# Last batch tile of a DLRM tower: the previous tile's late stages in the turn phase, and two column chunks multiplied ahead of the third one's turn

## What is computed

```python
e = jnp.stack([tbl_f[ids[:, f]] for f in range(27)], axis=1)   # 2048 x 27 x 128
inter = jnp.einsum('bfd,bgd->bfg', e, e)[:, triu_i, triu_j]     # 351 pairs
h = jnp.concatenate([e.reshape(B, -1), inter, dense_ctx], axis=1)  # 3456 + 351 + 16
h = jnp.maximum(h @ W_top1 + b_top1, 0.0)                       # 512
h = jnp.maximum(h @ W_top2 + b_top2, 0.0)                       # 256
y = h @ W_top3                                                  # 1
```

## Time and profile before

| | us |
|---|---|
| median of 3 runs | 601.06 (599.7 to 602.52) |
| the profiled execution | 602.09 |
| its span, first to last instruction | 600.0 |
| TensorE busy | 537.2 (90% of the span) |
| VectorE busy | 349.6 (58%) |
| ScalarE busy | 233.9 (39%) |
| GpSimd busy | 418.9 (70%) |
| granted TensorE clock, mean | 0.989 of full |
| chain that ended last: TensorE, VectorE, ScalarE | 69%, 18%, 2% |

### The profile page before, as it was taken

The page is one execution under the profiler, slowest core; times in us unless marked ns, Lnnn a source line. Parts: engine busy times, 40 slices in busy tenths (PEclk is TensorE's granted clock), DMA queues, the critical chain, the costliest instruction groups (busy, mean ns, idle before and its releaser), DMA issues.

```text
span 600.0 us, 7903 instructions
## 1 busy us (share of the span) xinstructions
PE 537.2 (90%) x2576; PEld 480.6 (80%) x2576; DVE 349.6 (58%) x1165; ACT 233.9 (39%) x717; POOL 418.9 (70%) x438
## 2 busy tenths in 40 slices
PE   0757899998999999899999999999999999999896
PEld 0547788897988889798888879888888988888774
DVE  2653827558383746748274664828366483837854
ACT  2543335162433526143352615344261524335341
POOL 4777777777777777777777777777777777777000
PEclk9987899999999999999999999999999999999999
DMA  7673222122222212122222222221222212222000
GB/s 229 193 255 98 52 54 53 50 54 53 54 53 53 53 49 53 50 54 51 51 54 54 52 54 52 50 54 52 54 52 54 53 50 52 54 54 54 10 0 1
DMA packets 19435, 37.80 MB, mean 63 GB/s; under 512 B 7636, under 2 KB 8660, under 8 KB 19396
## 3 DMA queue, kind: packets, MB, share of 16 engines
q0 software_dynamic: 13824, 28.34, 18.4%
q1 hardware_dynamic: 5284, 8.72, 4.5%
q10 hardware_dynamic: 288, 0.26, 0.2%
HBM read 37.28 MB, written 0.01 MB: 62 GB/s over the span
## 4 chain that ended last, share of the span: by engine, by line
PE 69%; DVE 18%; POOL 4%; issue 4%; DMA 2%; ACT 2%; DVEq 0%
PE ps_acc L222 18%; PE ps_acc L223 14%; PE ps_acc L224 13%; DVE g_buf L487 9%; PE ps_gram L247 8%; PE ps_acc L259 8%; DVE g_buf L481 6%; PE ps_t L209 5%; POOL emb L196 4%; DVE emb_x L471 2%; PE ps_late L296 1%; DMA emb<-in_tbl,idx 1%; DMA idx<-in_ids 1%; PE ps_late L255 1%; ACT g_buf L423 1%
## 5 line engine op out<-in xcount | busy, mean ns | idle before, releaser
L196 POOL DMA_INDIRECT emb<-in_tbl,idx x432 | 418.3, 968 | 136.2 <-issue 129.5
L222 PE MATMUL ps_acc<-w_hi,emb_x 128*128 128x512 f32 x432 | 211.0, 488 | 21.4 <-DVE emb_x L471 21.4
L481 DVE COPY g_buf<-ps_gram 32x112 f32<-32x112 f32 x512 | 138.3, 270 | 91.1 <-PE ps_gram L247 81.0
L223 PE MATMUL ps_acc<-w_lo,emb_x 128*128 128x512 f32 x432 | 174.8, 405 | 0.0
L224 PE MATMUL ps_acc<-w_hi,emb_x 128*128 128x512 f32 x432 | 174.0, 403 | 0.0
L423 ACT ACTIVATE g_buf<-ps_gram 32x112 f32<-32x112 f32 x512 | 130.8, 256 | 91.7 <-PE ps_gram L247 87.2
L222 PEld LDWEIGHTS ps_acc<-w_hi,emb_x 128*128 128x128 f32 x432 | 130.7, 303 | 33.7 <-issue 21.2
L471 DVE TENSOR_TENSOR emb_x<-ps_t,emb_x 128x512 fp32r<-128x512 f32 (+1 forms) x112 | 74.5, 666 | 142.6 <-ACT emb_x L384 142.2
L223 PEld LDWEIGHTS ps_acc<-w_lo,emb_x 128*128 128x128 f32 x432 | 135.2, 313 | 2.6
L384 ACT ACTIVATE emb_x<-ps_t 128x512 fp32r<-128x512 f32 (+1 forms) x112 | 63.8, 583 | 180.3 <-PE ps_t L209 179.9
L224 PEld LDWEIGHTS ps_acc<-w_hi,emb_x 128*128 128x128 f32 x432 | 131.7, 305 | 1.0
(11 more groups left out here) (26 smaller groups left out, 119.5 us busy)
## 6 DMA issues: line engine op xcount, KB each, us to landing
g_buf<-in_W_top SPq DMA_DIRECT2D x27, 256.0 KB, 4.2
emb<-in_tbl,idx POOLq DMA_INDIRECT x432, 2.5
w_cols<-in_W_top SPq DMA_DIRECT2D x1, 512.0 KB
w<-in_W_top SPq DMA_DIRECT2D x1, 512.0 KB
w_cols<-in_W_top SPq DMA_DIRECT2D x1, 222.0 KB
idx<-in_ids SPq DMA_DIRECT2D x1, 216.0 KB, 5.4
b_rows<-in_b_top ACTq DMA_DIRECT2D x1, 128.0 KB, 4.9
w_rows<-in_W_top ACTq DMA_DIRECT2D x1, 128.0 KB, 6.0
```

Source lines behind the costliest of these rows:

```text
L196: pool.indirect_dma_start(out=emb[:, f * D:(f + 1) * D], out_offset=None, in_=tables[f], in_offset=bass.IndirectOffsetOnAxis(ap=idx[:, t, ...
L222: pe.matmul(acc, emb_part(0, f), w_hi[:, f, :], start=(f == 0), stop=False)
L223: pe.matmul(acc, emb_part(0, f), w_lo[:, f, :], start=False, stop=False)
L481: last = dve.tensor_copy(target, source)
```

## The change

It touches the last tile alone. On TensorE the late stages of tile 14 leave their places between the gram units (before units 2, 6, 10 and 14): the turn of its columns goes ahead of the turn of group 5, their product behind that turn and two multiplies, the turn of its hidden layer behind the turn of group 6, and layer 2 ahead of unit 10. ScalarE takes tile 14's columns ahead of split 5, its ReLU ahead of split 6, and the copy of the turned hidden layer behind that. VectorE packs tile 14's pairs one group earlier. The tile's own multiplies are dealt out anew: two each ahead of units 0, 3 and 6. The wait for s_h2 moves from behind the remaining multiplies to ahead of them. At the end eight multiplies, the turn of chunk 0, one multiply, the turn of chunk 1, two multiplies, the products of chunks 0 and 1, then turn and product of chunk 2.

```diff
--- before.py
+++ after.py
@@ -269,12 +269,10 @@
                     last = turn_chunk(n, ps_late[:, n * P:(n + 1) * P])
                 last.then_inc(s_cols_t, 1)
 
-            def turn_last_columns(t):
-
-                pe.wait_ge(s_h2, t)
-                for n in range(NCC):
-                    pe.wait_ge(s_cols, t + 1 + n)
-                    turn_chunk(n, ps_gram[:, n, 0:P]).then_inc(s_cols_t, 1)
+            def turn_last_chunk(t, n):
+
+                pe.wait_ge(s_cols, t + 1 + n)
+                turn_chunk(n, ps_gram[:, n, 0:P]).then_inc(s_cols_t, 1)
 
             def multiply_columns(t):
                 pe.wait_ge(s_cols_out, t + 1)
@@ -284,11 +282,11 @@
                     last = multiply_chunk(t, n)
                 last.then_inc(s_acc, 1)
 
-            def multiply_last_columns(t):
-                for n in range(NCC):
-                    pe.wait_ge(s_cols_out, t + 1 + n)
-                    last = multiply_chunk(t, n)
-                last.then_inc(s_acc, 1)
+            def multiply_last_chunk(t, n):
+                pe.wait_ge(s_cols_out, t + 1 + n)
+                last = multiply_chunk(t, n)
+                if n == NCC - 1:
+                    last.then_inc(s_acc, 1)
 
             def turn_h1(t):
                 pe.wait_ge(s_h1, t + 1)
@@ -347,24 +345,34 @@
                 for _ in range(count):
                     multiply(t, todo.pop(0))
 
-            for g, count in ((2, 4), (3, 2), (4, 2), (5, 1), (6, 1)):
-                turn_group(t, g)
-                multiply_next(count)
+            turn_group(t, 2)
+            multiply_next(4)
+            turn_group(t, 3)
+            multiply_next(2)
+            turn_group(t, 4)
+            multiply_next(2)
+            turn_columns(t - 1)
+            turn_group(t, 5)
+            multiply_next(2)
+            multiply_columns(t - 1)
+            turn_group(t, 6)
+            turn_h1(t - 1)
             for k in range(UNITS):
-                if k == 2:
-                    turn_columns(t - 1)
-                if k == 6:
-                    multiply_columns(t - 1)
+                if k in (0, 3, 6):
+                    multiply_next(2)
                 if k == 10:
-                    turn_h1(t - 1)
-                if k == 14:
                     layer_2(t - 1)
-                if k in (3, 5, 8, 9, 12, 13):
-                    multiply_next(1)
                 gram_unit(t, k)
-            multiply_next(len(todo))
-            turn_last_columns(t)
-            multiply_last_columns(t)
+            pe.wait_ge(s_h2, t)
+            multiply_next(len(todo) - 3)
+            turn_last_chunk(t, 0)
+            multiply_next(1)
+            turn_last_chunk(t, 1)
+            multiply_next(2)
+            multiply_last_chunk(t, 0)
+            multiply_last_chunk(t, 1)
+            turn_last_chunk(t, 2)
+            multiply_last_chunk(t, 2)
             turn_h1(t)
             layer_2(t)
 
@@ -443,16 +451,15 @@
                 for k in range(0, UNITS, 2):
                     take_blocks(t, k)
             t = TILES - 1
-            for g in range(NG):
+            for g in range(5):
                 split_group(t, g)
+            take_columns(t - 1)
+            split_group(t, 5)
+            relu_h1(t - 1)
+            split_group(t, 6)
+            take_h1(t - 1)
             for k in range(0, UNITS, 2):
                 take_blocks(t, k)
-                if k == 4:
-                    take_columns(t - 1)
-                if k == 8:
-                    relu_h1(t - 1)
-                if k == 12:
-                    take_h1(t - 1)
             take_last_columns(t)
             relu_h1(t)
             take_h1(t)
@@ -549,10 +556,10 @@
             layer_3(t - 2)
             split_group(t, 3)
             add_parts(t - 1)
+            pack_pairs(t - 1, 0, 10)
             split_group(t, 4)
-            pack_pairs(t - 1, 0, 10)
+            pack_pairs(t - 1, 10, NF - 1)
             split_group(t, 5)
-            pack_pairs(t - 1, 10, NF - 1)
             split_group(t, 6)
             for k in range(1, UNITS, 2):
                 take_blocks(t, k)
```

## The result

The changed kernel takes 605.61 us in the median of 6 runs (601.95 to 608.45), the kernel before 601.11 in 6. The ratio is 1.0071 with a 95% interval of 1.0045 to 1.0096: slower, by 0.7%. Forecast were 603.7 us and a range of 601.0 to 606.7. The profiled execution took 605.6 us with a span of 603.7.

The account below looks back on a forecast made before the run. VectorE's last block copy, plus 10.9 us to the end of the columns product, was taken to set the end. That product ending at 595.8 instead of 593.2 gave +2.6 us: 603.7 on the median's basis, range 601.0 to 606.7.

Parts of the forecast that it names:

- first place: TensorE's 2.6 us wait at 560.7 for tile 14's packed columns; a clock fall behind it priced at 1.5 us.
- Part 1: Turn phase: TensorE waits 2.6 us for tile 14's packed columns; gram unit 0 starts at 571.0, against 564.40.
- Part 2: Gram phase: VectorE's last block copy ends at 583.5, 1.2 us later than 582.34.
- Part 3: Wait for s_h2 ahead of the multiplies: TensorE idles 2.0 us, counted at 0 because chunk 0 is packed only at 589.8.
- Part 4: End of the last tile: TensorE has a backlog, and the columns product ends at 595.8, against 593.2.
- The sum: Whole kernel: +2.6 us on the profiled 602.09 gives 604.7, or 603.7 on the basis of the median.
- the likeliest case: The forecast itself: 603.7 us, from the order alone with no clock fall; chance 0.50.
- rival (a): TensorE's clock falls behind one or both long waits in the last tile: 605.2 or 606.7 us; chance 0.32.
- the second place: Stretch 579.8 to 584.0: TensorE issues three gram units and idles 3.5 us; a clock fall there priced at 1.5 us.
- (b): Nothing changes: gram phase nearer the copies' pace, last copy between 580.9 and 582.3, median 601.1 to 602.5; chance 0.13.
- (c): Faster: VectorE runs the gram phase without a gap, last copy before 580.9; 598.0 us; chance 0.05.

Follow-up runs that it names:

- changed, again: The changed kernel run again, unaltered, as base of the other experiments: median 606.28 us, ratio 1.0089 to the kernel before.
- wait for s_h2 late: The changed kernel with the wait for s_h2 moved from ahead of the last eleven multiplies to ahead of the hidden layer's turn: 604.94 us, ratio 1.0072.
- old end: The changed kernel's turn and gram phase with the kernel before's end: eleven multiplies, wait for s_h2, three turns, three products: 601.74 us, ratio 1.0014.
- second wait filled: The changed kernel plus 11 unread matmuls of 512 columns behind gram units 12, 14 and 15: 603.52 us, ratio 1.0039.
- both filled: The changed kernel with 11 unread matmuls behind gram units 12, 14, 15 and ten ahead of the turn of tile 14's columns: 603.26 us, ratio 1.0055.
- first filled: The changed kernel with only the ten unread matmuls ahead of the turn of tile 14's columns: 605.34 us, ratio 1.0079.
- before, new end: The kernel before with only the changed kernel's TensorE end, from the wait for s_h2 to chunk 2's product: 603.44 us, ratio 1.0034.
- before, wait early: The kernel before with only the wait for s_h2 moved ahead of the eleven multiplies: 602.37 us, ratio 1.0019.
- staggered end: The kernel before, ending: eleven multiplies, turns of chunks 0 and 1, product 0, turn 2, products 1 and 2, then wait for s_h2: 600.65 us, ratio 0.9988.
- with layer 3 late: The staggered end plus VectorE's layer 3 of tile 14 moved behind the last packs: 600.53 us, ratio 0.9997 to the kernel before.
- waits used: Staggered end and late layer 3, plus four of the tile's own multiplies moved into TensorE's four waits: 600.76 us, ratio 1.0004 to the kernel before.
- waits used, filled: Waits used, plus seven unread matmuls ahead of chunk 0's turn; on another chip 724.98 us against 725.95 for the kernel before, ratio 0.9931.

## Why the prediction was right, and where not

Each stretch is from one profiled execution, in us.

| kernel | stretch expected, clock at full | measured | clock fell in it |
|---|---|---|---|
| before | | 46.7 | no |
| changed, first profile | 49.3 | 51.9 | 6.8 us |
| changed, again | 49.3 | 49.4 | no |
| wait for s_h2 late | 49.3 | 49.5 | no |
| old end | 47.9 | 47.9 | no |
| second wait filled | 49.3 | 51.1 | 3.4 us, first place |
| both filled / first filled | 49.4 / 49.4 | 49.5 / 49.5 | no |
| before, new end | 48.1 | 49.9 | 3.4 us |
| before, wait early | 47.6 | 47.9 | no |
| staggered end | 46.0 | 46.1 | no |
| with layer 3 late | 45.4 | 46.2 | no |
| waits used | 44.9 | 47.0 | 3.4 us |
| waits used, filled (another chip) | 45.2 | 45.3 | no |

**Part 1** held to 0.2 us: wait 2.51 for 2.6, gram unit 0 at 571.15 for 571.0.

**Part 2** held: last copy at 583.5, as walked unit by unit, though the waits ahead of units 13 and 15 were 0.70 and 0.30 us for 0.95 and 0.6. What it costs by itself is the 1.2 us of the kernel with the old end.

**Part 3** held, with a wait of 1.75 us for 2.0: moved late, the wait for s_h2 gives back nothing (49.5 beside 49.4), since TensorE stands at chunk 0 instead. What is left for it to cost in the changed order is the clock, and with 3 of 6 runs marked when it stands late and 9 of 12 when it stands early, the runs are too few to tell how much of that is the wait's. On the kernel before, the same early wait costs 1.2 us.

**Part 4** held: TensorE issues the last turn behind four records of L259 and doesn't wait for VectorE. In the changed order the new end costs 1.6 us (47.9 to 49.5). Put on the kernel before, it costs 1.6 as well without the clock, but 1.2 of them are the early wait. That two chunks multiplied early would win where TensorE has no backlog was worked out in the prediction and not run; one chunk multiplied early, with all eleven multiplies ahead of the turns, gave 0.6 us of stretch (46.7 to 46.1). The multiplies put behind the turns are such a backlog.

**The sum**, +2.6, was measured as 2.7 where the clock held. The direction was right and the range holds the time, but the likeliest case was not the commonest: I gave rival (a) 0.32, and 9 of the changed kernel's 12 runs show its mark. The median of 605.6 lies beside the 605.2 of (a) with one fall, not beside the forecast's 603.7, so the range holds it thanks to the rival's share of it. The fall was at the second place that (a) names: on the clock of the rows before it lasts from 582.9 to 589.7.

Two terms of (a) were off. *Its chance:* I held against it that waits of 1 to 1.2 us did nothing and that it was seen once. At the second place three waits (0.70, 0.30 and 1.75 us in the trace, 2.75 in all where I had walked 3.5) follow each other with only three gram units between; each alone is shorter than tile 1's 2.64. Filling them lowered the median by 2.8 us. *Its length:* I took the length of one fall, 3.4 us as in tile 1, and 1.5 lost. For that length the price is right: falls of 3.4 us cost 1.6 in two other kernels. But in the changed kernel's trace the fall lasted 6.8 us and cost 2.4. That 605.2 came so close is partly luck, since a smaller price stood in for runs of which some fell and some did not. Filling the first place, with the longest single wait, gave nothing that the times show, though I had priced it like the second. Why isn't settled.

The Trainium skill (page "TensorE: Matmul & The Clock Gate", section "Loop structure matters more than you think") has it that matmuls which follow each other keep the clock and that a long wait between them lets it go. Its example is a wait for a DMA; here the clock fell behind waits of 1.7 and 2.5 us on VectorE too, in some executions and not in others. In direction the rule was a better guide than the short waits of the trace, but it would look for the fall behind the longest wait, and four of five profiles show none there.

Rivals (b) and (c) needed a last copy before 582.3; it came at 583.5.

## What to carry over

When work is moved out of a stage, follow the engine that is last there to its end: here the gram phase began 6.7 us later (571.15 against 564.40), and its last copy ended 1.2 us later, not earlier. A step put in front of ready work, like a wait or the turn of a chunk not yet packed, blocks everything behind it in the queue; the leftover multiplies belong ahead of it. And read idle time of TensorE twice: as time, and as what the clock does behind it. If dense matmuls stand behind a wait, on the path that ends last, look at the clock of several executions, not of one.

## What the runs showed of the hardware that was not expected

Matmuls that nobody reads made the kernel faster: 11 of them in TensorE's waits took the median from 606.28 to 603.52 us. The clock's fall is a matter of the execution: one program with the same waits, the last of 1.75 us, showed 0.50 over 6.8 us in one profile and 1.00 in another. In the last tile falls came in lengths of 3.4 and 6.8 us, behind a wait of 2.51, behind one of 1.67 and 0.32 after it, behind a series of 0.70, 0.30 and 1.75, and once amid the short waits of the last stages (0.37 to 0.69 us each), where the one trace of before shows none. A wait of 1.67 us on the kernel before was followed by no fall in its profile. What decides was not isolated.
